# Head loop of a one-core network: the third and fourth query groups of the next pass turned and split at other places, nine unread TensorE products left out

## What is computed

```python
q  = concat([cq @ Wq_nope, rope(cq @ Wq_rope)])          # 16 heads x 64
o1 = attn(q, k1, v1, causal)                             # all earlier tokens
o2 = attn(q, ks, vs)                                     # 256 selected tokens
o3 = attn(q, kw, vw, causal & (i - j < 64))              # a window
o  = g[0] * o1 + g[1] * o2 + g[2] * o3
return o @ Wproj                                         # added to the tokens
```

## Time and profile before

| what | value |
|---|---|
| median of 3 runs | 2735.08 us (2731.08 to 2741.87) |
| profiled execution, span from first to last instruction | 2741.1 us |
| TensorE busy | 2453.0 us, 89% |
| VectorE busy | 1883.0 us, 69% |
| ScalarE busy | 1459.0 us, 53% |
| GpSimd busy | 1308.2 us, 48% |

### The profile page before, as it was taken

How to read it: one execution, slowest core, us unless ns; L and a number is a source line. 1 busy time by engine, 2 the same in 40 slices (tenths; PEclk the granted TensorE clock), 3 DMA queues, 4 the chain that set the end, 5 groups by cost and what they waited for, 6 DMA issues and landing times. The chain is left out here.

```text
span 2741.1 us, 52000 instructions
## 1 busy us (share of the span) xinstructions
PE 2453.0 (89%) x16743; PEld 1695.4 (62%) x16743; DVE 1883.0 (69%) x3715; ACT 1459.0 (53%) x2524; POOL 1308.2 (48%) x884
## 2 busy tenths in 40 slices
PE   5499996855899999999999999999999999999857
PEld 3366663544566666666666666666666666666755
DVE  2767763677476776867768677687776776867626
ACT  1114552332366657666576665766657666566323
POOL 0213782000246647457375573755737547366435
PEclk8699997967999999999999999999999999999779
DMA  3004210011431121111211202112021120212233
GB/s 113 1 6 93 62 33 9 1 46 58 106 90 43 36 52 35 43 45 26 52 35 43 56 15 52 35 43 56 15 52 35 43 56 15 52 35 47 76 109 97
DMA packets 85075, 131.56 MB, mean 48 GB/s; under 512 B 16224, under 2 KB 60768, under 8 KB 84624
## 3 DMA queue, kind: packets, MB, share of 16 engines
q1 hardware_dynamic: 81328, 123.16, 17.9%
q0 software_dynamic: 3024, 7.43, 0.9%
q10 hardware_dynamic: 656, 0.09, 0.0%
HBM read 63.49 MB, written 20.79 MB: 31 GB/s over the span
## 5 line engine op out<-in xcount | busy, mean ns | idle before, releaser
L2498 ACT ACTIVATE a_PT<-PS 128x512 f32<-128x512 f32 (+1 forms) x1111 | 613.6, 585 | 353.3 <-PE PS L2363 227.8
L2216 POOL TENSOR_TENSOR a_KT<-a_PT 128x512 f32<-128x512 f32 (+2 forms) x179 | 418.5, 2354 | 473.9 <-ACT a_PT L2498 464.8
L2216 POOL TENSOR_TENSOR a_KT<-a_KT,a_PT 128x2048 f32<-128x2048 f32 (+3 forms) x128 | 391.8, 3061 | 8.8
L2567 DVE TENSOR_REDUCE a_NM<-PS 128x2 fp32r<-128x512 f32 x460 | 296.8, 686 | 127.2 <-PE PS L2311 123.6
L2357 PE MATMUL PS<-a_QH,a_KSW 128*128 128x256 f32 (+2 forms) x848 | 287.5, 358 | 13.2 <-DVE a_NM L2567 12.5
L2357 PE MATMUL PS<-a_QH,a_K 128*128 128x512 f32 (+3 forms) x768 | 295.4, 395 | 0.0
L2581 DVE TENSOR_REDUCE a_MX<-PS 128x1 f32<-128x512 f32 (+3 forms) x432 | 265.7, 664 | 34.3 <-PE PS L2322 19.8
L2358 PE MATMUL PS<-a_QL,a_K1B 76*128 76x512 f32 (+3 forms) x768 | 259.6, 348 | 0.0
L2322 PE MATMUL PS<-a_K,a_QH 128*128 128x512 f32 (+3 forms) x768 | 254.7, 407 | 1.6
L2554 DVE TENSOR_TENSOR a_KSW<-PS,a_KSW 64x512 fp32r<-64x512 f32 x170 | 117.2, 690 | 124.2 <-ACT a_KSW L2457 121.0
L2308 PE MATMUL PS<-a_KSW,a_QH 128*128 128x512 f32 x460 | 198.6, 480 | 3.5 <-DVE a_QL L2551 3.5
(11 more groups left out here) (435 smaller groups left out, 5368.9 us busy)
## 6 DMA issues: line engine op xcount, KB each, us to landing
a_KWB<-a_KSW SPq DMA_DIRECT2D x68, 256.0 KB, 3.3
a_K1B<-a_K SPq DMA_DIRECT2D x32, 512.0 KB, 5.3
a_XC<-latents SPq DMA_DIRECT2D x17, 512.0 KB, 3.9
a_CKS<-latents SPq DMA_DIRECT2D x17, 512.0 KB, 4.6
a_CF<-latents SPq DMA_DIRECT2D x17, 448.0 KB, 4.1
slots<-in_empty_slots SPq DMA_DIRECT2D x1, 5160.0 KB, 19.7
f_XB<-slots SPq DMA_DIRECT2D x8, 645.0 KB, 4.1
c_EX<-in_experts SPq DMA_DIRECT2D x1, 4608.0 KB, 17.6
```

What stands on the lines that cost most here:

```text
L2216: nc.gpsimd.tensor_tensor(total, one_in, other_in, ALU.add).then_inc(s["added"], 1)
L2498: nc.scalar.activation(PT[:, to:to + width], turning(key)[:, 0:width], ACT.Exp).then_inc(s["taken"], 1)
L2567: ins = nc.vector.tensor_reduce(out, bank.rearrange("p (a n) -> p a n", a=2), AX.X, ALU.max, negate=True)
```

## The change

Three things. (1) `tr.q2` and `tr.q3` with their splits, which opened a pass, now belong to the steps done ahead at the end of the pass before: `tr.q2` between the score tiles 1.0 and 1.1, `tr.q3` after the values of tile 3 and ahead of `sum.0`; their splits stand ahead of `norm.0` on VectorE. (2) The other steps of the pass's end are dealt out between the score tiles too: `tr.w3` ahead of tile 0's second part, `a.q3` after it, `v.vw.1` and `v.vs.0` further on, and GpSimd's `rope.q3` ahead of `add.0`. (3) The nine products before `near.4.0` are gone.

```diff
 ORDER = """
-wk tr.q2 tr.q3 split.tr.q2 split.tr.q3
+wk
 score.4.0
 score.4.1 v.v1.0 near.4.0
...
-+score.0.0 +turn.0.1 value.22.22 add.18 value.23.23 value.24.24 add.19 +rot.w3 add.20 sum.5 norm.5
-+score.0.1
-+score.1.0
-+score.1.1
-+score.2.0
-+score.2.1
-+score.3.0 +rope.w3 +v.vw.1 +rope.q2 ysum.5 +v.vs.0 +tr.w3 +split.tr.w3 +a.q3 +rot.q3 +double.w3 project.5 +value.0.0 +value.1.1 +value.2.2 +add.0 +add.1 +value.3.3 +add.2 +add.3 +sum.0 +rope.q3 +norm.0
++score.0.0 +turn.0.1 value.22.22 add.18 value.23.23 value.24.24 add.19 +rot.w3 add.20 sum.5 norm.5 +rope.w3 +tr.w3 +split.tr.w3
++score.0.1 +a.q3 +rot.q3
++score.1.0 +rope.q2 +tr.q2 +split.tr.q2
++score.1.1 +v.vw.1
++score.2.0 +double.w3
++score.2.1 +v.vs.0
++score.3.0 ysum.5 +rope.q3 project.5 +value.0.0 +value.1.1 +value.2.2 +add.0 +add.1 +value.3.3 +add.2 +add.3 +tr.q3 +split.tr.q3 +sum.0 +norm.0
 """
...
                     after(pe, q, at, bank_free(key, q))
-                    if i == 4 and h == 0:
-                        keep_clock(9, bank)
                     after(pe, q, at, *(("reduced", ("split", "tr", g)) for g in made))
```

## The result

The changed kernel takes 2791.77 us in the median (2782.64 to 2794.42) against 2735.33 us of the kernel before beside it: a ratio of 1.0199, interval 1.0178 to 1.022, 2% slower. The forecast was 2750, its range ended at 2768. The profiled execution of the changed kernel, the shortest of its four, has a time of 2782.64 us and a span of 2780.4 us.

A forecast was written before the change was run, and what follows sets the result against it. TensorE was taken to bound the head loop. Boundaries 15 x 0.6, edges +2.6 and clock falls +3.1 gave +14.7 us on 2735.1, so 2750 us, range 2738 to 2768.

The forecast's parts named there:

- The chain: From `tr.q3` through ScalarE's copies, VectorE's split and transpose to `near.4.0`: each boundary about 0.6 us longer.
- the clock: TensorE's granted clock falls at 8 of 15 boundaries, each costing 0.8: +6.4, less 3.3, so +3.1 us.
- The two old falls: Slow stretches at two boundaries of the kernel before, up to 1.65 us each; 3.3 us subtracted for them.
- the edges: Last pass 4.1 us longer, once; prologue gains 1.5 of the wait for weights WP: +2.6 us.
- The nine products: Unread products before `near.4.0`, 1.34 us per boundary, counted in the 3.0 us taken out.
- The clock at every boundary: Rival: the clock falls at all 15 boundaries at the full 1.65 us each: 2768 us; chance 0.14.
- The clock that never falls: Rival: idles this short never lower TensorE's clock: 2743 us; chance 0.18.
- The wait that really goes: Rival: `norm.0`'s transpose ends before `score.4.0`, nothing stands between `v.v1.0` and `near.4.0`: 2689 us; chance 0.05.

The follow-up runs named there:

- fill_both: Changed kernel with unread products in both new waits, ten ahead of `sum.0`'s, nine ahead of `score.4.1`'s: 2745.51 us, 1.0029 of the kernel before.
- nine_out: Kernel before with its nine unread products left out and no step moved: 2751.06 us, 1.0047 of the kernel before.
- q3_late: Changed kernel with q2 turned after `score.3.0` and q3 turned and split after `near.4.0` of the next pass: 2734.1 us, 0.9974 of the kernel before.
- q3_split_first: `q3_open` with VectorE's split of q3 ahead of `near.4.0` and `wk` behind `near.5.0`: 2695.5 us, 0.9836 of the kernel before.
- split_behind: Changed kernel with VectorE's split of q3 moved behind `norm.0`: 2800.9 us, 1.0227 of the kernel before.
- nine_back: Changed kernel with the nine unread products put back ahead of `near.4.0`, behind both new waits: 2791.47 us, 1.0192 of the kernel before.
- fill_sum: Changed kernel with ten unread products ahead of `sum.0`'s wait only, `score.4.1`'s wait left bare: 2763.37 us, 1.011 of the kernel before.
- q3_open: `q3_late` with q3 turned as first product of a pass, its split behind `near.4.0` and `wk` on VectorE: 2751.87 us, 1.0051 of the kernel before.

## Why the prediction was wrong

- **The chain was right.** `tr.q3` starts 10.94 us behind 1427.07 and `score.4.1` 16.26; forecast were 10.9 and 16.2. The waits stand at the places named, 0.25 + 1.49 + 1.44 = 3.2 us, for 0.4 + 2.0 + 1.2 = 3.6 forecast. At full clock the boundary is 0.6 us longer (`fill_both`): 15 x 0.6 = 9.
- **The step that failed is the clock:** "I take a fall at 8 of 15 boundaries, each at 0.8, half the old price because part of the slow time lies in waits (bounds 0 and 1.65)". Measured: 15 falls at 2.6 us, 39 us for 6.4. The halving went the wrong way. The two old falls lasted 3.4 us each; the new ones last 6.8. Most do begin in the wait, but TensorE then works from 1443.33 to 1448.8 at half speed, 5.5 us, which by estimate loses half of that, some 2.7. The upper bound, taken from two rows behind a single wait, was no bound for two waits, so the range was too short at its upper end.
- **The sum of the loop.** 9 + 39, less 3.8 for the two passes with the old falls (114.80 and 114.69), and 3.4 for the stop, is 47.6 us. From the first to the last residual the changed profile needs 47.5 us more (830.67 to 2600.57, against 835.19 to 2557.59). The medians differ by 56; the other 9 us were not placed. The stretch ahead of the first residual alone took 824 to 848 us in the profiles, and differed by 13 us between the two of the changed kernel; so the forecast's 2.6 for the edges can't be told from them either.
- **The nine products.** The sum counted their 1.34 us as saved and priced their absence only within the clock's term. `nine_out` shows that without them the kernel before falls at 13 boundaries, not 2.
- **The rivals.** The clock at every boundary came true, at 2.6 instead of 1.65, so 2768 was too low; it had 0.14. The clock that never falls, 2743 with 0.18, did not: falls came behind two waits of 1.5 us, and behind single ones of 1.4 to 2.05. By the rule of the Trainium skill (TensorE: Matmul & The Clock Gate, Why this matters for your kernels) only longer gaps worry. The traces differ among themselves: in `q3_late` 14 of 15 waits of 1.8 us passed without a fall, in `nine_out` only 2 of 15 waits of 1.75 to 2.05 us.
- **The wait that really goes**, with 0.05, did not come with this change. It came when q2 was turned early, q3 late and neither split stood ahead of the transpose or of what reads it: `near.4.0` then follows `sum.0` 3.5 us earlier than before (`q3_split_first`).

What decides a fall stays open. The waits below are those of over 1 us at the boundary:

| kernel | waits, us | products nobody reads | falls of 15 |
|---|---|---|---|
| before | 1.66 (1.95 at the three changes of batches) | nine behind | 2, both behind a 1.95 |
| `nine_out` | 1.75 (2.05 at the three changes) | none | 13 |
| changed | 1.49, 1.44 | none | 15, one at a stop |
| `split_behind` | 1.5, 1.9 to 2.4 | none | 15 |
| `nine_back` | 1.5, 1.5 | nine behind | 11, one at a stop |
| `fill_sum` | 1.4 | ten ahead, in the first wait | 5, two at stops |
| `fill_both` | none | ten and nine, in the waits | 0 |
| `q3_late` | 1.80 | none | 1 |
| `q3_open` | 1.91 | none | 8 |
| `q3_split_first` | none | none | 0 |

Here two waits were worse than one, and filled waits had no fall; but behind one wait of 1.75 the clock fell at 13 boundaries and behind one of 1.80, at another place, at 1. Length alone doesn't tell. Nor does the list of steps: in `nine_out` the falls begin anywhere from 0.3 us before the end of the wait to 2.0 us behind it, with the same instructions around it each time. So the moment at which a wait comes may decide, and no run moved a wait in time alone. Why stops show only in the kernels in which `score.4.1` waits wasn't tried either.

## What to carry over

A wait of an engine with a granted clock can cost the slow work behind it on top of its own length: here two waits of 1.5 us that replaced one wait and a filler cost 2.6 us more than the chain showed, so price a fall from its whole slow stretch and don't take an old fall for the upper bound. Before unread products are removed as waste, ask what stands idle beside them. When work is moved across a loop's edge, follow the bank that each moved step leaves and the next step that takes it: four of these kernels lost their gain to a ring position or to a neighbour in a list, and the two that lost none were 1.6% faster than the kernel before.

## Unexpected on the hardware

- Removing 1.34 us of TensorE work per pass made the kernel before slower, by 0.5% (`nine_out`).
- Falls of the clock came in two lengths, some 3.4 and 6.8 us (10 in four of the six passes with a stop), and cost from 0.9 to 3.0 us a pass (`nine_out`).
- TensorE stood for 6.2 to 6.6 us at some changes of batches while code was fetched, at one in one execution of the changed kernel and at two in another.
